# Another common order for the steps of three streams in a four-batch transformer kernel

## The reference

```python
x = _layernorm(x + L0_attn(x))   # causal latent attention of 16 heads of 8, then windowed (32) attention
x = _layernorm(x + L0_ffn(x))    # mixture of 8 experts, top 2, 128 -> 512 -> 128, gelu
x = _layernorm(x + L1_attn(x))   # linear attention, width 64, phi = elu + 1, running state
x = _layernorm(x + L1_ffn(x))    # twice: windowed attention (8 heads of 64, window 64), then a gated feed-forward
```

## Time and profile before

| | us |
| --- | --- |
| median of 3 runs (lowest, highest) | 1995.46 (1993.88, 2000.35) |
| span of the profiled execution | 2052.9 |
| TensorE busy in it | 1657.8 (81%) |
| ScalarE busy | 1219.5 (59%) |
| VectorE busy | 1103.2 (54%) |
| POOL busy | 786.1 (38%) |

### The profile page before, as it was taken

How to read it: one execution, slowest core, us unless ns; L and a number is a source line. 1 busy time by engine, 2 the same in 40 slices (tenths; PEclk the granted TensorE clock), 3 DMA queues, 4 the chain that set the end, 5 groups by cost and what they waited for, 6 DMA issues and landing times.

```text
span 2052.9 us, 37396 instructions
## 1 busy us (share of the span) xinstructions
PE 1657.8 (81%) x13911; PEld 1075.7 (52%) x13911; DVE 1103.2 (54%) x2039; ACT 1219.5 (59%) x2805; POOL 786.1 (38%) x654
## 2 busy tenths in 40 slices
PE   3865488887877998988887897899788895788786
PEld 2234355435665665634665664634665673456463
DVE  4124601538766545766776344665775344665573
ACT  3752266545645897477645886389555772265572
POOL 2530423326342455166225345266216223152440
PEclk7896588869988998999888998899999997789997
DMA  5000343011021432011012341011003440010110
GB/s 153 1 1 1 108 128 100 3 50 39 20 73 62 118 109 56 6 40 25 17 52 75 118 124 33 6 30 24 17 26 105 123 128 21 18 40 17 32 25 11
DMA packets 64214, 109.54 MB, mean 53 GB/s; under 512 B 12463, under 2 KB 37283, under 8 KB 63907
## 3 DMA queue, kind: packets, MB, share of 16 engines
q1 hardware_dynamic: 58339, 98.23, 16.3%
q0 software_dynamic: 4096, 8.40, 1.4%
q10 hardware_dynamic: 1600, 0.52, 0.1%
HBM read 74.40 MB, written 15.93 MB: 44 GB/s over the span
## 4 chain that ended last, share of the span: by engine, by line
PE 48%; DVE 19%; ACT 15%; issue 8%; POOL 4%; DMA 2%; another core or an unknown queue 2%; SPq 0%; ACTq 0%; DVEq 0%; POOLq 0%
PE PX L863 5%; PE PX L1256 4%; PE PX L1189 4%; PE PX L1276 4%; PE PX L1088 4%; ACT back_arena L1565 3%; PE PX L1210 3%; ACT middle_arena L1513 2%; PE PX L1099 2%; PE PX L911 2%; ACT front_arena L1400 2%; PE PX L1200 2%; PE PX L1312 2%; POOL front_arena L2270 2%
## 5 line engine op out<-in xcount | busy, mean ns | idle before, releaser
L1400 ACT ACTIVATE front_arena<-PX 128x1024 f32<-128x1024 f32 (+3 forms) x352 | 271.1, 825 | 110.5 <-PE PX L911 84.2
L2270 POOL TENSOR_TENSOR front_arena<-front_arena,tri 128x256 f32<-128x256 f32 x234 | 184.0, 801 | 358.9 <-ACT front_arena L1400 358.7
L2333 POOL TENSOR_TENSOR back_arena<-back_arena 128x512 f32<-128x512 f32 x128 | 191.4, 1501 | 320.3 <-DVE back_arena L2128 319.9
L1256 PE MATMUL PX<-wqkv,hT 128*128 128x512 f32 x384 | 217.9, 660 | 25.8 <-ACT back_arena L1565 12.4
L1565 ACT ACTIVATE back_arena<-PX,fnm 128x128 f32<-128x128 f32 x512 | 181.7, 373 | 94.2 <-DVE fnm L2135 93.2
L2338 POOL TENSOR_TENSOR fy<-fm,minus_half 128x16 f32<-128x16 f32 x64 | 191.7, 2995 | 64.8 <-DVE fm L2151 63.1
L863 PE MATMUL PX<-front_arena 128*32 128x512 f32 (+3 forms) x1408 | 172.5, 557 | 30.5 <-POOL front_arena L2270 20.8
L2135 DVE TENSOR_REDUCE fnm<-PX 128x4 f32<-128x512 f32 x128 | 88.3, 690 | 150.8 <-PE PX L1276 142.7
L911 PE MATMUL PX<-front_arena 32*128 32x512 f16 (+3 forms) x768 | 122.8, 356 | 33.3 <-ACT front_arena L1400 13.4
L1276 PE MATMUL PX<-back_arena 64*64 64x128 f32 x2048 | 143.5, 280 | 0.2 <-ACT back_arena L1603 0.2
L1276 PEld LDWEIGHTS PX<-back_arena 64*64 64x64 f32 x2048 | 111.7, 135 | 50.9 <-issue 49.8
(11 more groups left out here) (303 smaller groups left out, 3592.6 us busy)
## 6 DMA issues: line engine op xcount, KB each, us to landing
W<-in_W SPq DMA_DIRECT2D x44, 514.0 KB
middle_arena<-in_W SPq DMA_DIRECT2D x39, 514.0 KB
back_arena<-back_arena SPq DMA_DIRECT2D x128, 128.0 KB, 2.4
xpos<-x_tables SPq DMA_DIRECT2D x64, 128.0 KB, 2.0
y_rows<-middle_arena SPq DMA_DIRECT2D x20, 256.0 KB, 5.5
back_arena<-in_W SPq DMA_DIRECT2D x9, 514.0 KB
middle_arena<-x_rows SPq DMA_DIRECT2D x8, 512.0 KB, 4.4
x_tables<-back_arena SPq DMA_DIRECT2D x1, 2048.0 KB, 7.5
```

The costliest lines, as they stand in the source:

```text
L1256: pe.matmul(p, hT[:, 128 * i:128 * i + 128], wqkv[:, l, c:c + 512], start=True, stop=True).then_inc(filled(b, "f" + n, l, i), 1)
L1400: act.activation(pb[:, :, 0:n], p[:, :, 0:n], ACT.Exp, scale=INV_SQRT_HD).then_inc(freed(b, "S", half, g, kc, jp), 1)
L2270: pool.tensor_tensor(pb, pb, tri[:, :].unsqueeze(1).to_broadcast([128, 2, 128]), ALU.mult).then_inc(sg("masked"), 1)
L2333: pool.tensor_tensor(T1[k % 2][:, hs, :], T1[k % 2][:, hs, :], T2[:, hs, :], ALU.add).then_inc(sg("rot"), 1)
```

## The change

The table `RUNS` is replaced by another table for the same steps. The order inside each stream is the same, since each stream's steps are numbered; every instruction, wait and buffer is kept; only where a step of one stream stands among those of the others differs, and with it the order of the instructions of different streams in each engine's queue, and the PSUM slots that follow from it. The table has one line more, so that all lines below it stand one line further down than before.

```diff
 RUNS = """
-F156 M2 F1 M1 F1 M1 F1 M3 F1 M1 F1 M2 F3 M1 F1 M4 F3 M1 F2 M1 F4 M1 F1 M3
...
-M1 B1 M2 B2 M1 B1 M3 B1 M1 B212
+F153 M1 F4 M3 F3 M4 F5 M1 F1 M2 F1 M1 F4 M4 F4 M1 F1 M1 F1 M5 F1 M4 F2 M3
...
+M2 B1 M1 B1 M2 B1 M2 B1 M1 B212
 """
```

More of the change, by code:

```diff
@@ L330 @@
-M1 B11 M1 B4 M1 B1 M2 B1 M1 B6 M3 B6 M4 B8 M2 B8 M3 B5 M2 B7 M2 B5 M2 B7
-M2 B5 M4 B1 M1 B7 M2 B1 M2 B3 M2 B2 M1 B1 M1 B1 M1 B1 M1 B1 M1 B1 M2 B1
-M1 B1 M2 B2 M1 B1 M3 B1 M1 B212
+F153 M1 F4 M3 F3 M4 F5 M1 F1 M2 F1 M1 F4 M4 F4 M1 F1 M1 F1 M5 F1 M4 F2 M3
+F11 M3 F1 M3 F2 M1 F2 M6 F1 M1 F8 M1 F1 M1 F1 M1 F3 M3 F5 M1 F2 M1 F1 M1
+F1 M1 F3 M1 F6 M1 F3 M1 F3 M1 F1 M2 F3 M1 F1 M1 F1 M1 F4 M1 F4 M1 F2 M1
+F3 M1 F18 B2 F1 B1 F2 B1 F1 B2 F2 B4 F1 B2 F1 B2 F1 B2 F2 B1 F1 B2 F1 B11
+F1 B3 F1 B7 F1 B5 F1 B4 F1 B5 F3 B1 F1 B1 F2 B3 F1 B2 F1 B2 F2 B2 F3 B1
@@ new lines @@
+F2 B1 F1 B2 F1 B6 F1 B1 F1 B4 F1 B3 F1 M1 F1 M3 B3 F1 M1 B1 M1 B1 F1 M1
+B2 F2 M1 B1 M1 B3 F1 B1 M1 B1 M2 B1 M1 B1 F1 M1 F1 B2 M1 B1 F1 M1 B2 F1
+M2 B1 M1 F2 M1 B1 M1 B1 F1 M1 B2 F1 M1 B1 M1 B1 F1 B2 F1 B4 F1 B2 M1 B1
+M1 B5 M1 B1 M1 F1 B1 F1 B1 F2 B2 F1 M1 B1 M1 F2 B3 F1 B2 F1 B5 M1 B1 M2
+B2 F1 B3 F1 B1 F1 B1 F1 M2 B1 F2 B4 F1 M1 B1 M1 F1 B1 F2 B2 F1 B1 M2 B1
+F2 B2 F2 B3 M1 B1 M1 F1 B1 F1 B1 F1 M1 B1 M2 F2 B4 M1 B1 F1 B2 M1 F1 B3
+M1 B2 M1 B1 F1 B1 M3 B6 F1 B2 F1 M1 F2 B1 M1 F1 M1 B2 M1 F1 M1 B3 F1 B1
@@ new lines @@
+F1 M1 F1 M2 B1 M1 B2 F1 M1 B1 M2 F1 B1 F2 B3 M1 B2 M1 F1 M1 B2 M1 F2 B1
+F3 B1 F1 B1 F1 B1 F1 B3 F1 B1 F4 B3 F1 B1 F1 B2 F1 B1 F2 B1 F1 B1 F1 B2
+F2 B2 F2 B1 F4 B3 F1 B2 F2 B1 F1 B2 F1 B1 F2 B1 F1 B3 F4 B1 F1 B1 F2 B2
+F2 B2 F1 B1 F2 B1 F1 B1 F3 B1 F4 B3 F1 B1 F1 B3 F1 B3 F1 B2 F4 B2 F1 B1
+F4 B3 F1 B1 F1 B2 F1 B1 F2 B1 F4 B1 F2 B1 F4 B5 F1 B1 F1 B1 F1 B3 F1 B3
+F1 B1 F2 B2 F1 B1 M1 B1 F1 M1 F1 M1 B2 M1 F1 B3 M1 F1 B1 F1 B1 M1 B1 M1
+B1 F1 M1 B1 F1 M1 F1 M2 B2 F1 M1 B4 F1 B1 M1 B2 M1 B2 M1 B3 F1 B2 M1 B3
@@ new lines @@
+M1 B1 F1 M1 B1 M1 B1 M2 B1 M1 B1 F1 B2 F1 M2 B1 F1 B1 F2 B2 M2 B2 F2 B1
+M2 B1 F1 B1 F1 B1 F1 B1 M1 B1 M1 F1 B8 M1 F1 B2 M2 B3 F1 B1 F1 B1 M2 B4
+F2 B1 M2 B1 F1 B5 M2 B4 F1 B3 F1 B1 M2 B6 M1 B1 M1 F1 B1 M1 F1 M1 B2 M1
+B2 F1 M1 B4 M1 B1 M1 F1 B5 M1 B1 M2 B1 F1 B2 M2 B1 F1 M1 F2 B1 M1 F1 B2
+F1 M1 F1 M1 B2 M1 F1 M2 B1 M1 B2 F1 M1 F1 B3 F1 M1 B1 F1 B1 M1 B1 M1 F3
+B1 F2 M1 B2 F2 B2 F1 B2 F1 B1 F2 B1 F3 B2 F3 B4 F3 B1 F3 B1 F2 B1 F1 B1
+F2 B1 F1 B1 F1 B2 F2 B3 F2 B1 F1 B1 F1 B2 F2 B2 F1 B2 F3 B1 F1 B1 F5 B1
@@ L333 @@
+F1 B1 F1 B1 F2 B2 F2 B4 F1 B1 F2 B1 F1 B1 F1 B3 F4 B2 F1 B2 F2 B1 F2 B1
+F4 B3 F3 B3 F1 B2 F8 B3 F5 B1 F3 B1 F2 B1 F6 B5 F1 B2 F2 B3 F1 B2 F1 B1
+F1 B5 F2 B2 M2 B2 M2 B1 M1 B2 M1 B2 M4 B2 M1 B7 M3 B1 M1 B4 M1 B4 M1 B5
+M1 B2 M1 B1 M2 B5 M2 B2 M1 B4 M2 B7 M2 B7 M2 B8 M3 B4 M1 B1 M1 B8 M2 B5
+M2 B7 M2 B5 M3 B2 M1 B4 M4 B5 M2 B2 M1 B2 M2 B1 M1 B1 M1 B1 M1 B1 M2 B2
+M2 B1 M1 B1 M2 B1 M2 B1 M1 B212
 """
```

## The result

The new order is slower. Its four runs have a median of 2067.64 us (2056.79 to 2079.52) against 1994.67 for the kernel before; the ratio is 1.036, with a 95% interval of 1.032 to 1.040. That is 73 us more, where I had forecast 6 us less, and outside the range. One execution, of e18, took 4439 us and stands in no ratio of this document.

What follows compares the result with a forecast made beforehand. TensorE, busy 81% of the span, was taken as the bound, with only its idle time open to change. The terms summed to -6.4 us of the profiled 2052.9, scaled to -6.2: 1989 us, range 1981 to 1997.

Steps and rivals of the forecast that it cites:

- batch 1's scatters: Sixteen DMAs on POOL split after ten: w2 matmuls 7.5 us sooner, less later waits; together -3 us.
- batch 2's gathers: POOL's runs of 4 and 12 DMAs become 4, 6 and 6, removing two thirds of TensorE's gaps: -4.5 us.
- the rival by the DMA: TensorE loses the same for each DMA wherever it stands, so splitting runs saves nothing: 2001 us, chance 0.15.
- Its busy time has no reason to move.: Premise on TensorE: no instruction is added or taken away, so only its idle time, 395 us, can change.
- Batch 0's scatters: Six of the sixteen DMAs go behind the first causal mask, so expert transposes wait for scattered rows: +5 us.
- The slower rival: POOL's in-order queue becomes the bound, scatters standing behind work that waits: 2005 us, 2000 to 2012, chance 0.20.
- Small distances: In six places a step and its source become neighbours, at half a microsecond each: +3 us.
- The back stream's setup: Moved behind all score steps, so ScalarE's 11.53 us table wait no longer holds TensorE 3.77 us: -3.8 us.
- Batch 3's experts: Late weights at hidden step 4 cost 6.9 us; that goes, a wait up to 4.2 comes at step 3: -2.7 us.
- the projection: Linear attention's output projection in two batches no longer directly follows the transposes that feed it: -2.4 us.
- Function tables: ScalarE switches its function table 98 times instead of 93, at 1.28 us a load: +2 us.
- the other runs: POOL's DMA runs in batch 0's and 1's gathers and batch 2's scatters: one grows, two shrink, 0 us.

Runs made afterwards that it cites:

- e18: Kernel before with the back stream's setup behind the last score steps and batch 3's experts' hidden steps 3 and 4 moved later: ratio 0.9978.
- e1: The kernel before, unchanged, run and profiled again: 2000.09 us, ratio 1.0008.
- e8: Kernel before with the new order only in 54 steps around batch 1's routing and scatters: ratio 1.0034.
- e5: Kernel before with the new order only in the 36 steps around batch 0's scatters: ratio 1.0060.
- e13: Kernel before with 130 unused transposes on TensorE ahead of batch 1's fourth score unit: ratio 1.0033.
- e6: Kernel before with the new order up to the back stream's start, except the 36 steps around batch 0's scatters: ratio 1.0058.
- e10: Kernel before with only the back stream's setup moved behind the last ten score steps: 1990.85 us, ratio 0.9953.
- e7: Kernel before with the new order only from the back stream's start to batch 1's routing, 121 steps: ratio 1.0034.
- e14: Kernel before with the new order only from batch 1's first expert pairs to the end of batch 0's back stream, 210 steps: ratio 1.0042.
- e15: Kernel before with the new order only from the start of batch 2's back stream to the end of batch 3's attention, 200 steps: ratio 1.0056.
- e16: Kernel before with the new order only from batch 3's routing on: ratio 1.0015.
- e17: Kernel before with the back stream's setup moved and the linear attention's output projection one step later in batches 0 and 2: ratio 0.9995.
- e11: Kernel before with the back stream's setup, the linear attention's projection in batches 0 and 2, and batch 3's experts' hidden steps moved: ratio 1.0003.

## Why the prediction was wrong

- **The row of the profile that I took as the base.** The sum was made against 2052.9 us and scaled by 0.972. The difference was not a scale: it was an execution with stalls that no other trace has. Two gains stood on them, batch 1's scatters (-7.5 of the -3) and batch 2's gathers (-4.5). Neither existed; e1 and e8 show it. Had they been left out, the sum would have been +5.6, the rival by the DMA. A third term used them too: the first mask of batch 0 was put at 251.2 because a stall of 8.27 us was to end sooner.
- **"Its busy time has no reason to move."** This is the step that failed most: 46.7 of the 79.6 us by the pair of profiles, 42 by the means of the stretches. The rivals kept it too, and the slowest of them ended at 2012 us. The matmuls are the same, but the granted clock fell from 0.895 to 0.877; the four timed runs have 0.877 to 0.885, and those of the kernel before that stand beside the experiments 0.886 to 0.903. e5 and e13 show at one place that the clock stays low behind a wait and is high behind work of like length. The Trainium skill, "TensorE: Matmul & The Clock Gate", section HAM oscillation — how this bites in real kernels, describes waits between groups of matmuls after which each group starts slow; the traces of e5 and e13 agree (0.51 behind the wait, 1.00 behind the work). That all of the slower matmuls come from longer waits is not shown, and e6, which waited less at a lower clock, speaks against so simple a rule: what in the order sets the clock in each stretch stays open.
- **Batch 0's scatters, +5.** The queue was the right one and the times came within 2 us, but in part by luck, since the mask stands at 252.7 with the old order too; the size was wrong: 12 us alone (e5). TensorE meets the wait for the second mask before it comes to the expert transposes, the only place that I had checked, and 3 to 5 us of slower matmuls came with it. The sign of being wrong that I had named, masks that hold TensorE for more than 5 us, came true with 7.66. The slower rival named this queue, but with a first mask later than 254 as its cause; the mask came at 252.75 and the cost came all the same.
- **Small distances, +3.** The largest mis-sized term. I had counted six neighbours and taken half a microsecond each. Matmul by matmul over the two traces, TensorE's idle time before it grew by over 0.8 us at 56 places, 84 us in all, and shrank by as much at 36, 53 us in all; e10, where one step moved, differs from e1 by as much at 8. Batch 0's scatters are 7.4 of the 84; the next are 3.9 at the layernorm ahead of batch 0's second gated half (7.50 against 3.63), 3.2 at batch 3's queries and 3.0 at a mask, and the other 52 are under 2.7. They lie also where I had priced nothing (e7, e14, e15).
- **The back stream's setup, -3.8.** Right in the mechanism: the wait is gone, and its stretch is 4.0 us shorter in e10. In the time it shows in e10 (0.9953) and not beyond doubt in the three that add moves to it.
- **Batch 3's experts, -2.7, and the projection, -2.4.** The waits went, and the new wait at hidden step 3 did not come in the kernel after; the time did not follow (e16, e17). In e11's trace most of what was saved comes back at the next waits of the queue.
- **Function tables, +2, and the other runs, 0.** The trace has the 98 loads against 93, 1.28 us each; what of them shows in the time no experiment isolates, nor what the other runs cost.
